# Order of the dense products in a turn of the second block: first feed-forward products two a step, second layer in the last four steps

## The reference, cut to what matters

```python
qkv = (x @ qkv_w).reshape(b, n, 3, H, D)
q, k, v = jnp.moveaxis(qkv, 2, 0)
scores = jnp.einsum('bhnd,bhmd->bhnm', q, k) * scale
scores = jnp.where(mask, scores, -jnp.inf)
attn = jax.nn.softmax(scores, axis=-1)
out = jnp.einsum('bhnm,bhmd->bhnd', attn, v)
attn_out = out @ proj_w + proj_b
x = x + gate_msa * _modulate(_layernorm(attn_out), shift_msa, scale_msa)
mlp_out = jax.nn.gelu(x @ fc1_w + fc1_b, approximate=False) @ fc2_w + fc2_b
x = x + gate_mlp * _modulate(_layernorm(mlp_out), shift_mlp, scale_mlp)
```

## Time and profile before

| | |
|---|---|
| time, median of three runs | 1455.85 us |
| time of the profiled execution | 1457.03 us |
| its span | 1455.2 us |
| TensorE matmul busy | 1309.6 us (90%) |
| VectorE, ScalarE, GpSimd busy | 55%, 53%, 52% |
| mean granted clock of TensorE | 0.978 |
| turn 8 begins, turn 15 ends (near) | 886 us, 1405 us |

### The profile page before, as it was taken

The page is one execution under the profiler, slowest core; times in us unless marked ns, Lnnn a source line. Parts: engine busy times, 40 slices in busy tenths (PEclk is TensorE's granted clock), DMA queues, the critical chain, the costliest instruction groups (busy, mean ns, idle before and its releaser), DMA issues. The chain is left out here.

```text
span 1455.2 us, 24552 instructions
## 1 busy us (share of the span) xinstructions
PE 1309.6 (90%) x8789; PEld 1004.0 (69%) x8789; DVE 803.2 (55%) x2240; ACT 770.5 (53%) x1262; POOL 757.1 (52%) x939
## 2 busy tenths in 40 slices
PE   4898999999999999999999997989888898988777
PEld 3676777777777777777777775666666666665556
DVE  3766645645646656656645643464655556454452
ACT  3565665665665765665655752544544353453522
POOL 3788876776776776776776761020413222140323
PEclk9999999999999999999999998999999999999988
DMA  8432222223213213213213215353424242433100
GB/s 258 130 127 57 71 84 72 73 75 83 74 64 89 75 58 88 78 55 88 79 54 110 92 41 164 113 152 108 151 67 145 61 155 93 123 116 86 45 2 29
DMA packets 98259, 133.98 MB, mean 92 GB/s; under 512 B 16802, under 2 KB 51498, under 8 KB 98130
## 3 DMA queue, kind: packets, MB, share of 16 engines
q1 hardware_dynamic: 96850, 131.80, 30.3%
q10 hardware_dynamic: 1280, 0.53, 0.2%
HBM read 72.64 MB, written 58.75 MB: 90 GB/s over the span
## 5 line engine op out<-in xcount | busy, mean ns | idle before, releaser
L617 POOL TENSOR_SCALAR shifted<-shifted,row_max 128x512 f32<-128x512 f32 x512 | 360.6, 719 | 220.1 <-DVE row_max L1380 218.2
L1380 DVE CUSTOM_DVE_ANT_0 shifted<-score,bias 128x512 f32<-128x512 f32 x512 | 332.7, 687 | 255.4 <-PE score L855 165.6
L1091 ACT ACTIVATE probs<-turned 128x512 f32<-128x512 f32 x512 | 278.2, 596 | 211.4 <-PE turned L867 209.8
L867 PE MATMUL turned<-ident,shifted 128*128 128x128 f32 x2048 | 270.0, 275 | 6.8 <-POOL shifted L617 6.0
L867 PEld LDWEIGHTS turned<-ident,shifted 128*128 128x128 f32 x2048 | 233.6, 141 | 55.6 <-issue 26.6
L783 PE MATMUL dense<-w_down,hidden 128*128 128x256 f32 x1024 | 253.3, 383 | 0.8 <-ACT hidden L1072 0.8
L610 POOL TENSOR_SCALAR bias<-dist,scale 128x1024 f32<-128x1024 f32 x192 | 220.0, 1146 | 13.6 <-DMA down_bias<-in_L_cond_b 13.6
L855 PE MATMUL score<-k_rows,q_rows 97*128 97x512 f32 x512 | 205.2, 456 | 22.1 <-DVE row_max L1380 10.1
L783 PEld LDWEIGHTS dense<-w_down,hidden 128*128 128x128 f32 x1024 | 185.6, 191 | 32.6 <-issue 9.6
L763 PE MATMUL dense<-feat_m,w_up 128*128 128x512 f32 x768 | 188.4, 400 | 3.5 <-ACT hidden L1072 1.8
L763 PEld LDWEIGHTS dense<-feat_m,w_up 128*128 128x128 f32 x768 | 144.3, 192 | 37.1 <-ACT hidden L1072 5.3
(11 more groups left out here) (138 smaller groups left out, 1497.3 us busy)
## 6 DMA issues: line engine op xcount, KB each, us to landing
qk_rows<-qk_high SPq DMA_DIRECT2D x128, 256.0 KB
q_rows<-qk_rows SPq DMA_DIRECT2D x64, 384.0 KB
qk_rows<-qk_low SPq DMA_DIRECT2D x64, 256.0 KB
k_rows<-qk_rows SPq DMA_DIRECT2D x68, 192.0 KB
x_in_t<-in_x SPq DMA_DIRECT2D x8, 512.0 KB, 3.8
x_res<-in_x SPq DMA_DIRECT2D x8, 512.0 KB, 5.5
x_mid<-x_norm SPq DMA_DIRECT2D x8, 512.0 KB, 3.3
x_in_t<-x_mid SPq DMA_DIRECT2D x8, 512.0 KB, 3.9
```

The source lines that it names most:

```text
L617: ins = pool.tensor_scalar(shifted[:, u % 3, i, :], shifted[:, u % 3, i, :], -1.0, row_max[:, t % 6:t % 6 + 1], ALU.mult, ALU.add)
L867: mm = pe.transpose(turned_bank[z % 2][:, HALF * kk + P * i:HALF * kk + P * i + P], shifted[:, u % 3, i, P * kt:P * kt + P], ident[:, :])
L1091: act.activation(probs[:, u % RING, 2 * pair:2 * pair + 2, :], turned_bank[z % 2][:, :].rearrange("p (a c) -> p a c", a=2), ACT.Exp)\
L1380: dve.tensor_tensor_reduce(shifted[:, u % 3, i, :], score_bank[t % 2], bias[:, u % 2, i, :], 1.0, 3.0e38, ALU.add, ALU.min, row_max[:, t % ...
```

## The change

The tables for a turn of the second block are written anew. `qk3` comes ahead of `t2` (places 7 and 9 in place of 8 and 7); the `up` pieces stand two a step in steps 4 to 7 in place of four a step in steps 3 and 4; the second layer stands in steps 8 to 11, in place of steps 5 to 11. On ScalarE the GELUs of the four pieces of steps 4 and 5 all stand at place 16 (step 5), and those of steps 6 and 7 at place 22 (step 7). On VectorE `peaks_of` comes ahead of the `add_tile` calls in step 2. No instruction is added or taken away.

```diff
     HEADS = {0: [("v", 3), ("t3", 0), ("t3", 1)], 1: [("t1", 0), ("t1", 1)], 2: [("wout", 0), ("wout", 1)],
-             3: [("wout", 2), ("wout", 3), ("qk", 0)], 5: [("qk", 1)],
-             6: [("qk", 2)], 7: [("t2", 0), ("t2", 1)], 8: [("qk", 3)],
-             10: [("up", 0), ("up", 1), ("up", 2), ("up", 3)], 13: [("up", 4), ("up", 5), ("up", 6), ("up", 7)],
-             19: [("down", 0)], 23: [("down", 1)], 28: [("down", 2)], 35: [("down", 3)]}
+             3: [("wout", 2), ("wout", 3)], 4: [("qk", 0)], 5: [("qk", 1)], 6: [("qk", 2)], 7: [("qk", 3)],
+             9: [("t2", 0), ("t2", 1)], 13: [("up", 0), ("up", 1)], 16: [("up", 2), ("up", 3)],
+             19: [("up", 4), ("up", 5)], 22: [("up", 6), ("up", 7)], 26: [("down", 0)], 29: [("down", 1)],
+             32: [("down", 2)], 35: [("down", 3)]}
+    HEADS_GELU = {16: (13, 16), 22: (19, 22)}
     HEAD_STEPS = H // 2 + 4
-    HEADS_DOWN = {16: (0, 4), 17: (4, 6), 19: (6, 9), 20: (9, 11), 22: (11, 14), 23: (14, 16), 25: (16, 19),
-                  26: (19, 21), 28: (21, 24), 29: (24, 25), 31: (25, 28), 34: (28, 29), 35: (29, 32)}
+    HEADS_DOWN = {25: (0, 6), 26: (6, 8), 28: (8, 14), 29: (14, 16), 31: (16, 22), 32: (22, 24), 34: (24, 28),
+                  35: (28, 32)}
...
             def turn(n):
                 if short(n):
+                    later = [k for group in HEADS_GELU.values() for k in group]
                     for p in range(HEAD_STEPS):
                         for k in range(3 * p, 3 * p + 2):
-                            for piece, m in pieces(HEADS, k, n):
-                                dense(piece, m)
+
+                            for x in HEADS_GELU.get(k, () if k in later else (k,)):
+                                for piece, m in pieces(HEADS, x, n):
+                                    dense(piece, m)
...
                         for piece, m in pieces(HEADS, 3 * p, n):
                             dense(piece, m)
+                        if 2 <= p < 2 + H // 2:
+                            peaks_of(n, p - 2)
                         if p == 2:
                             if n == B:
                                 first_norm("norm", 1, n - 1)
                             else:
                                 for t in range(TT):
                                     add_tile(n - 1, 0, t)
-                        if 2 <= p < 2 + H // 2:
-                            peaks_of(n, p - 2)
```

## The result

The changed kernel takes 1508.07 us (median; 1507.05 to 1514.29), against 1455.59 us for the kernel before measured beside it: a ratio of 1.036, with an interval of 1.033 to 1.039. The forecast was 1492 us within 1464 to 1510. Of its own profiled execution the span is 1506.4 us, 51.2 more than before.

The account below looks back on a forecast made before the run. TensorE, busy 90%, bounds the kernel, so only its waits and clock count: 2.8 + 2.1 = 4.9 us in turns 9 to 14 (29.4), 3.5 each in turns 8 and 15 (7), together 36, hence 1492 us, range 1464 to 1510.

Parts of the forecast that it names:

- Part 1 and 2: Steps 2 and 3, `qk3` before `t2`, `t2` at place 9: TensorE waits of 1.6, 2.1 and about 3.1 us a turn.
- Part 4: Second layer in steps 8 to 11: waits of 0.7 and 1.0 us for maxima and 0.6 before the last `attend_heads` go.
- Part 3: Steps 4 to 7, `up` two a step, GELU twice a turn: `up3` waits 1.0 us and `up7` 1.1 for banks.
- The clock: Pair 1's scores to first `up` at 1.2 GHz: 3.4 us extra against 1.3 now, 2.1 us more a turn.
- The late traffic: Output and loads on SP some 7 us later in the turn, meeting pair 3's maxima: priced at no change.
- the rival: Late traffic holds up pair 3's maxima in six turns, 2.5 us each: 15 us more, 1507 us; chance 0.10.
- The rival without further loss of clock (1475): Waits in the turns as worked out, but no further clock loss: 19 us more, 1475 us; chance 0.17.
- the faster one (1440): VectorE is not late in steps 2 and 3, so steadier steps 4 to 11 win: 1440 us; chance 0.08.
- The sign to look for: Step 3's turned maxima wait about 3 us; the forecast is wrong if they wait less than 1.5 us.
- the port: Step 4: GpSimd holds VectorE's subtraction of the maxima 2.4 us, costing 1.2 us in eight turns: 1502 us; chance 0.05.

## Why the prediction was right, and where it was off

**Part 1 and 2 of the working held.** The pauses of steps 2 and 3 were worked out as 1.6, 2.1 and 3.1 us and are 1.58, 2.13 and 2.95. Laying VectorE's queue beside TensorE's, row by row, was enough for that. Turn 15, where the earlier trace rows showed 1.00 us, now waits 1.42. The run with `t2` at place 10 confirms the cause of the third.

**Part 4 held.** In turn 12 TensorE waits for nothing between 1224 us and the end of the turn.

**Part 3 was mis-sized: 1.0 and 1.1 us were 1.72 and 1.64.** The chain from the end of step 4 to the GELU of `up0` left out one instruction. ScalarE, turn 12, steps 4 and 5:

```profile
1204.71 0.64 ACTq L1114 DMA_DIRECT2D q_rows<-peaks  x1
1205.45 1.09 ACT L1108 ACTIVATE probs<-turned 128x512 f32<-128x512 f32 x2 [5.60 <-PE turned L925]
1206.56 1.28 ACT L1073 ACT_TABLE_LOAD   x1
1207.85 1.85 ACT L1073 ACTIVATE hidden<-dense,up_bias 128x512 f32<-128x512 f32 x3
```

`load_peaks` stands ahead of `head_exp` and holds ScalarE for 0.64 us, about the difference; no run moves this issue, so it is read from the rows. It does not count as busy, and so it was left out. Over eight turns these waits are 28.3 us in sixteen, where 2.1 us a turn, 16.8, were worked out: 11.5 us too few, of which sixteen issues of 0.64 us are 10.

The load itself costs 1.28 us and is followed at once by the GELU, as in the earlier trace rows. The drain of 1.38 us that the Trainium skill (ScalarE: Activation LUTs, What ACT_TABLE_LOAD costs) gives is not seen in this trace either.

**The clock was mis-sized.** The extra loss was put at 2.1 us in turns 9 to 14 and at little in turns 8 and 15. It is 2.1 in turns 11, 12 and 14, where the clock falls once, but 3.2 on the mean of the six, and turn 15 loses 7.6 us where it lost 2.6. The assumption that a turn whose clock had fallen already can't lose more held in turn 8 (6.0 us, was 5.8) and was wrong in turn 15, whose time at 1.2 GHz went from 6.8 to 20.5 us with the longer pauses. That is some 7 us over turns 9 to 14 and at least the 3 us by which turn 15 went beyond its 3.5.

**The late traffic was priced at no change, and the rival came true in part.** The "issue" waits are 8.3 us in five turns against 4.1 in eight waits before, and 2.33 us in turn 12, which had 0.2. Moving the loads gave 9 us. The rival's bound of 2.5 us in six turns was too high, the forecast's nothing too low.

**What the working did not see.** It gave steps 4 to 11 a gain, 2.1 us of waits in place of 3.5, and laid the loss on steps 2 and 3. The sum was nearly right, the division was not: the wait of step 3 was written under `t2`, but it has two causes, `t2` in VectorE's queue and the four `up` pieces taken out of TensorE's. Each brings a wait by itself, as the two half changes show: 1.61 us before the first `up` with steps 2 and 3 changed alone, 2.48 us before the turned maxima with steps 4 to 11 changed alone. The first half costs 26 us alone, the second, which should have gained, 46.

The rival without further loss of clock (1475) and the faster one (1440) fell. The first of them was also summed wrongly: the forecast holds 2.1 us of clock in six turns and 0.7 in two, 14 us, and the rival takes off 16.8; it should have read 1478. The sign to look for was named, a wait of step 3 under 1.5 us, and it was 2.95. The mis-sized terms are 11.5 us for the waits for a GELU, 7 and 3 for the clock and some 4 for the DMA, 25 to 26 us. Against them stand some 5 us for `t2`'s transposes, which the working did not credit: 20 to 21, where the miss was 16. Turn 8 had a wait of 4.2 us for `x_norm` before and has none after, in no term of the sum, which is about what is left over; that it is the same time is not shown.

So the time lies in the range in part by luck. The narrower range, 1482 to 1502, was missed, and the wide one was held by 2 us because the terms that were too small were partly met by others that the working did not have.

## What to carry to other kernels

In a kernel whose busiest engine is fed by chains across three others, dense work is cover, and a spread that looks more even takes it from the places that need it: write the queue of each engine beside the others before a piece is moved, with the issues of DMAs in it, since they hold an engine while counting as idle. A longer table-switch count can be cheaper than a late GELU, if it is the GELU that frees a bank. And after every wait that is taken away, look for the next one behind it: here the DMA of the maxima and the port took back a part of several gains.

## What the runs showed of the hardware

- A subtraction of two 8-column operands in SBUF on VectorE took 2.36 us in place of 0.17 when GpSimd had begun a long instruction 0.03 us earlier, and so in seven turns of the run with filled pauses. In the run in which GpSimd starts one `up` piece later it was held over 2 us in one turn only. This agrees with the Trainium skill (SBUF — State Buffer, Who interferes with whom), by which an instruction of VectorE with two SBUF inputs meets a GpSimd instruction that reads SBUF. In the kernel before, the rows showed it only for a cast (1.85 us).
- In the changed kernel a DMA of 8 KB was issued at 1211.81 us, and the wait for it ended at 1218.36, 6.5 us later, while the output, two loads of 512 KB and the rows of a group, issued from 1209.43 on, were under way.
- At like work the time at 1.2 GHz grew from 3.4 us a turn or less to 10 to 17 us (turns 9 to 14) by three pauses of 1.6 to 3 us with 0.3 and about 2 us of work between them, and matmuls whose results nobody reads brought the mean clock from 0.954 to 0.989.
